# A gather ring of 24 tiles in place of 16, in a graph network kernel on one core

## The reference, cut to what matters

```
W = einsum('rb,bio->rio', comp, basis)          # 8 relations
H = einsum('ni,rio->nro', x, W)                 # a table of 20000 rows of 256
msg = H[src, etypes]                            # one row per edge: the gather
agg = segment_sum(msg, dst, num_segments=2500)  # "the first sums"
out = agg + x @ loop_weight + bias
```

## Time and profile before

| what | value |
|---|---|
| median of 3 runs | 1731.75 us |
| lowest and highest of them | 1726.88 and 1733.42 us |
| span of the profiled execution | 1668.6 us |
| mean granted clock of PE in it | 0.923 of full speed |
| PE, PEld, DVE busy | 1495.7, 1005.9, 1028.6 us |
| ACT, POOL busy | 615.6, 781.2 us |

### The profile page before, as it was taken

How to read it: one execution, slowest core, us unless ns; L and a number is a source line. 1 busy time by engine, 2 the same in 40 slices (tenths; PEclk the granted TensorE clock), 3 DMA queues, 4 the chain that set the end, 5 groups by cost and what they waited for, 6 DMA issues and landing times. The chain is left out here.

```text
span 1668.6 us, 23723 instructions
## 1 busy us (share of the span) xinstructions
PE 1495.7 (90%) x6795; PEld 1005.9 (60%) x6795; DVE 1028.6 (62%) x2542; ACT 615.6 (37%) x1534; POOL 781.2 (47%) x738
## 2 busy tenths in 40 slices
PE   4999788999999999998356799999999999999996
PEld 2554314665666777777233467767766767767785
DVE  6543244345445555545388789898898888896432
ACT  3121002333234343443022355554555445555341
POOL 1100277646755777600378666574746556540000
PEclk9999857999999999999556699999999999999997
DMA  8448456546766566631487885665757565641100
GB/s 258 164 161 261 142 151 172 154 115 191 213 175 180 166 190 178 164 94 47 137 252 216 267 253 165 193 180 167 208 152 212 143 196 169 179 122 39 29 7 9
DMA packets 191573, 270.07 MB, mean 162 GB/s; under 512 B 28295, under 2 KB 156035, under 8 KB 188867
## 3 DMA queue, kind: packets, MB, share of 16 engines
q1 hardware_dynamic: 148419, 144.77, 27.7%
q0 software_dynamic: 43008, 123.61, 26.8%
HBM read 196.22 MB, written 72.06 MB: 161 GB/s over the span
## 5 line engine op out<-in xcount | busy, mean ns | idle before, releaser
L1890 POOL DMA_INDIRECT att_kv<-table_kv,g_srcI x314 | 368.5, 1174 | 246.4 <-issue 180.4
L1149 POOL DMA_INDIRECT ex_hg<-table_h,z_idx x314 | 316.7, 1008 | 150.2 <-issue 84.9
L2441 PE MATMUL att_psR<-g_mw,att_h 128*128 128x256 f32 x640 | 163.9, 403 | 1.0 <-ACT att_h L2259 1.0
L2414 PE MATMUL att_psR<-att_t,g_mw 128*128 128x256 f32 (+1 forms) x640 | 154.8, 387 | 0.1
L1466 PE MATMUL ex_psG<-ex_hg,ex_oh 128*42 128x256 f32 x628 | 134.6, 427 | 13.3 <-DMA ex_hg<-table_h,z_idx 7.2
L751 PE MATMUL tab_psH<-e_u,tab_xT 128*128 128x512 f32 x320 | 142.6, 598 | 4.3 <-DVE e_u L532 4.3
L2441 PEld LDWEIGHTS att_psR<-g_mw,att_h 128*128 128x128 f32 x640 | 124.7, 200 | 23.0 <-ACT att_h L2259 4.0
L1387 ACT ACTIVATE ex_h<-ex_psH,g_cols 128x256 f32<-128x256 f32 (+1 forms) x240 | 97.3, 464 | 93.8 <-PE ex_psH L1488 93.1
L2414 PEld LDWEIGHTS att_psR<-att_t,g_mw 128*128 128x128 f32 x640 | 121.2, 199 | 16.6 <-issue 2.6
L1882 POOL DMA_DIRECT2D table_o<-att_part x59 | 54.2, 919 | 161.9 <-DMA table_o<-att_part 90.5
L2301 PE MATMUL att_psG<-att_kv,att_oh 128*42 128x264 f32 x628 | 109.5, 431 | 13.7 <-DVE att_kv L1997 13.3
(11 more groups left out here) (308 smaller groups left out, 2465.1 us busy)
## 6 DMA issues: line engine op xcount, KB each, us to landing
table_h<-tab_hs SPq DMA_DIRECT2D x20, 1024.0 KB, 4.0
att_eft<-in_eft SPq DMA_DIRECT2D x158, 64.0 KB
ex_db<-table_dst SPq DMA_DIRECT2D x79, 126.0 KB
table_ohT<-ex_ohT SPq DMA_DIRECT2D x79, 126.0 KB
att_ohT<-table_ohT SPq DMA_DIRECT2D x79, 126.0 KB
table_oh<-ex_oh SPq DMA_DIRECT2D x79, 84.0 KB, 2.3
att_oh<-table_oh SPq DMA_DIRECT2D x79, 84.0 KB, 4.0
table_kv<-ex_qkv SPq DMA_DIRECT2D x10, 512.0 KB, 4.8
```

What stands on the lines that cost most here:

```text
L1149: nc.gpsimd.indirect_dma_start(hg[:, t % RING0, :], None, d.h[:, :], bass.IndirectOffsetOnAxis(ap=g.idx0[:, t:t + 1], axis=0)).then_inc(go ...
L1890: nc.gpsimd.indirect_dma_start(kv[:, t % (RINGC * TP), H:H + 2 * D], None, d.kv[:, :], bass.IndirectOffsetOnAxis(ap=g.srcI[:, t:t + 1], ax ...
L2414: ins = nc.tensor.matmul(out[:, c * CB:c * CB + used(b)], g.mw1[:, e, k, c * P:(c + 1) * P], t3[:, k, 0:used(b)], start=(k == 0), stop=(k ...
L2441: ins = nc.tensor.matmul(out[:, q * D:(q + 1) * D], h1[:, n % 3, k, q * P:(q + 1) * P], g.mw2[:, e, k, :], start=(k == 0), stop=(k == DK - 1))
```

## The change

The ring has 24 slots in place of 16, with 24 `got` semaphores in place of 16 and 24 KB in place of 16 KB of each partition.

```diff
-RING0 = 16
+RING0 = 24
```

## The result

| | before | after |
|---|---|---|
| median of 20 runs each | 1728.16 us | 1738.82 us |
| lowest and highest | 1718.1 and 1755.43 us | 1725.94 and 1754.76 us |
| ratio, 95% interval | | 1.0057 [1.0037, 1.0078] |

All ratios here are of fast runs alone, which leaves out those over 1.5% above the fastest of the same kernel, so a ratio isn't exactly the quotient of two medians. The ring of 24 costs 10.7 us. It is a small loss, but the interval lies clear of 1. Forecast was no change at 1731 us; the measured time is inside the stated range, at the very end of it.

The account below looks back on a forecast made before the run. PE was taken to set the pace from 260 to 755 us, with the ring stopping nobody who matters. All terms were 0, so the 1731.75 us median stays, forecast as 1731 us, range 1724 to 1739 us.

Parts of the forecast that it names:

- What bounds the kernel: Stage of the first sums, 260 to 755 us: PE sets the pace, busy 486.26 of 495 us, 8.74 us idle.
- the ring never holds POOL: Up to 297 us POOL gathers without waiting on a full ring; the first long wait, 1.86 us, is at the 77th gather.
- The first 76 gathers: Start of the sums: gathers issue at POOL's own pace in both versions, so cost 0 and gain 0.
- Eight more slots hidden in POOL's idle time: After 297 us: filling takes 10 us of POOL's 58.6 us of waits, leaving about 48; gain 0 for PE.
- PE's waits for the gather: Up to 260 us: PE's 7.2 us of waits in 11 places for gathered rows stay as they are.
- Rival A: The ring starves PE at the start; the 7.2 us of waits go, giving 1724.5 us; chance 0.04.
- The traffic: DMA: same 314 gathers, only sooner; DVE's waits for destination rows may shift; taken as 0, ends plus and minus 7.2 us.
- Rival C: Shifted gather bursts delay DVE's destination rows and PE, 1739 to 1746 us, chance 0.04; or faster, 1724.5 us, chance 0.03.
- The joins: POOL's joins issue at the same time as before, with 17.6 us of slack at the tightest pair; cost 0.
- Rival B: Late joins stop DVE and through it PE, groups 54 to 78: up to 15 us, 1747 us; chance 0.03.
- The end: Last gather, at 701.0 us, comes up to two groups earlier, between 680 and 692 us; last join stays; nobody waits.
- The range: Whole kernel: 1724 us (ring starving PE) to 1739 us (first step of shifted bursts); chance of slower 0.05.

Follow-up runs that it names:

- c1: The kernel before, unchanged, run and profiled again: ratio 1.0013 to the kernel before, profiled span 1730.4 us.
- e2: The kernel before with 8 KB more in the ring's tile, unused: ratio 1.0000 to the kernel before.
- x8: The kernel before plus eight gathers in a row at tile 64, into slots nobody reads: ratio 1.0095 to the kernel before.
- c2: The changed kernel (ring of 24), unchanged, run again on another chip: ratio 1.0072 to the kernel before.
- r20: The kernel before with a ring of 20 slots in place of 16: ratio 1.0038 to the kernel before.
- r12: The kernel before with a ring of 12 slots in place of 16: ratio 0.9989 to the kernel before.
- e3: The changed kernel with the joins put back behind the same gathers as before: ratio 1.0096 to the kernel before.
- k2: 24 slots, used 24 deep only up to tile 64, then 16, joins as in the changed kernel: ratio 1.0206 to the kernel before.
- z8: The kernel before plus eight iotas of 128x256 on POOL at tile 64, without DMAs: ratio 1.0024 to the kernel before.
- e1: 24 slots and semaphores, but waits and joins as with 16 slots: ratio 1.0033 to the kernel before.
- k3: The kernel before, its ring of 16 used only 8 deep up to tile 64: ratio 0.9989 to the kernel before.
- s8: The kernel before plus eight unread gathers, one in every second group from tile 128 to 184: ratio 1.0027 to the kernel before.

## Why the prediction was wrong

**What bounds the kernel.** Right in the main for the long stretch: PE is by far the busiest engine from 260 to 755 us, though with 31 us of idle time in c1 and 30 in after, not 8.74. Wrong in the premise that "the ring never holds POOL" up to 297 us. That is so in the one trace, and not in c1 or e2, which run the same streams: there the ring is full by 231.1 us, and POOL's pause of 4.06 us is the moment in which PE's signal gets through. There the full ring doesn't harm PE by stopping POOL; it helps, since it ends POOL's row.

**The warning I explained away.** The profiled span lay 63.15 us under the median, and I called this "time around the first and the last instruction". It is 1.4 to 2.5 us in every run with both numbers. A gap of 3.7% between a profile and the runs it stands for meant that the profile showed another course of the kernel. The sum was made on a course without the holds, and of all timed runs of this kernel none took less than 1709.79 us.

**The first 76 gathers: cost 0.** This is the step that failed. There were 28 gathers and then a pause, and the change moved the pause behind the 36th. Cost: 10.2 us on POOL (241.3 - 231.1), 11.4 us at group 4, 12.0 us at group 50, 10.7 us in the timed runs. The prediction counted a gather in POOL's idle time as hidden, and had no term for what it does to PE's signals.

**Eight more slots hidden in POOL's idle time.** The waits of POOL for PE did not shrink to 48 us: 62.6 us in after, 65.8 us in the second profile of before. The slots had been filled in the first row already. The claim that ten more microseconds of POOL are "still not on PE's path" is what x8 contradicts most directly: it adds just those, reads nothing of them, and costs 0.95%.

**PE's waits for the gather.** They went from 1.6 to 0.9 us, not near the 7.2 us of the earlier trace rows, which again belong to the other course. Rival A (the ring starves PE) is false for this change: c2 and r20 are slower than 16 slots, and even r12 is no slower.

**The traffic.** Right for these waits. DVE waits 21.7 us in 10 places for `db` after, 7.2 us the longest, against 20.6 us in 11 before. Rival C is out, although its time, from 1739 us up, is nearly what came.

**The joins.** Right that they cost nothing here: DVE doesn't wait for them, group 50 to 78 takes 194.8 against 194.6 us, and e3 loses without the move. Rival B's mechanism exists and is dear, as k2 shows by 33 us, but it takes joins that wait for a later sum.

**The end.** The last gather was to come up to two groups earlier. It starts at 735.5 against 740.4 us: 4.9 us earlier, with the groups 12 us later, so it did gain nearly 17 us on the sums, somewhat over two groups.

**The range.** The time is inside it, 0.2 us from its end, and that is luck: the bound came from rival C, which is not what happened. The chance of 0.05 for slower was far too small: it priced waits of known kinds, and left out that a shared path might exist that the profile has no name for.

**What stays open.** Why signals of PE are held while POOL issues. PE's ends are modelled in the trace, so it can't be told whether PE finished late or its signal came late. It isn't all signals: in after DVE writes its masks from 227.75 us, and SP, which waits for them, stores them from 228.00 us, in the middle of POOL's row. Nor does every row hold a signal to its end: that of group 2 came in the middle of one, ACT copied the gates in z8 at 295.55 us in a row from 290.72 to 299.20 us, and the first profile had 76 gathers in a row and no hold. What decides this was not found. The profile itself names "remote", "issue" or a stale DMA as the releaser, never POOL. No run kept POOL busy for 10 us without DMAs. And the small loss of e1, and the missing gain of r12 and k3, are not explained.

## What to carry to other kernels

Compare the span of a profile with the timed runs before anything is built on it: if they differ by more than a few microseconds, profile the kernel again. Where an engine issues long rows of indirect DMAs, more buffers ahead are not free even if it has idle time: fill them a few at a time, and take the smallest ring that doesn't starve the consumer (here 12 or 16 tiles, where 8 starve PE and 20 or more cost time). That filling them a few at a time avoids the cost is argued from s8 and was not tried on the ring itself. Look for the hold by the start of the engine that waits for PE, not by the end that the trace models for PE.

## What the hardware did that I had not expected

While POOL issued indirect DMAs without a pause, consumers of PE's results started up to 22.5 us after the modelled end of the matmuls (244.21 against 221.71 us in c2; 246.34 against 225.85 us in after). In the holds at group 3, at `ex_h` and at the gates they woke 2.1 (c1, `ex_h`) to 5.3 us (k2, group 3) after the end of the row. Four gathers more in POOL's first row brought the copy of group 3 5.5 to 5.7 us later, a little more than four times their pitch of 1.25 us. Eight gathers more at tile 64 cost 11 to 16 us in the timed runs (0.66 to 0.95%), whether they moved 128, 16 or 8 KB each. Eight iotas (2.45 us of POOL in all), eight loads of 128 KB by SP, or the same eight gathers one at a time cost nothing that could be measured.
